# Context attention on 64-row halves with resident keys, and sums by a ones matmul

## The reference

```python
q = x_normed @ Wq + bq            # (2, 1024, 256), 16 heads of 16
k, v = ctx @ Wk + bk, ctx @ Wv + bv   # (2, 77, 256)
scores = q @ k.T / sqrt(16)       # first layer: k zeroed and a large negative number added where the mask is 0
p = softmax(scores, axis=-1)      # over 77 context tokens
out = (p @ v) @ Wo + bo
```

## Time and profile before

| | |
|---|---|
| Median of 3 runs | 3210.11 us (3195.41 to 3211.3) |
| The profiled execution | 3210.68 us, its span 3208.8 us |
| Stage `a1` | from 565.3 to 689.3 us |
| Stage `a4` | from 2064.4 to 2189.3 us |
| PE busy over the span | 2470.8 us, 77% |
| DVE busy over the span | 1611.6 us, 50% |
| ACT busy over the span | 1106.8 us, 34% |

### The profile page before, as it was taken

The page is one execution under the profiler, slowest core; times in us unless marked ns, Lnnn a source line. Parts: engine busy times, 40 slices in busy tenths (PEclk is TensorE's granted clock), DMA queues, the critical chain, the costliest instruction groups (busy, mean ns, idle before and its releaser), DMA issues. The chain is left out here.

```text
span 3208.8 us, 47429 instructions
## 1 busy us (share of the span) xinstructions
PE 2470.8 (77%) x16056; PEld 1352.3 (42%) x16056; DVE 1611.6 (50%) x2632; ACT 1106.8 (34%) x1993; POOL 923.3 (29%) x840
## 2 busy tenths in 40 slices
PE   4669975763899498799999996686479998419992
PEld 3524423332788375233333334544312222308882
DVE  3767725435223232566666662544679984412222
ACT  1326651330000133344444441142137887101110
POOL 0522232102000211477777772201612112030004
PEclk7969987575899799899999998767779999659996
DMA  3433213522565476122222213542432210154553
GB/s 106 100 71 84 70 25 76 87 56 85 182 208 184 132 194 179 64 83 81 80 83 81 84 59 106 104 80 71 101 58 62 59 36 16 43 174 165 194 190 111
DMA packets 280975, 322.77 MB, mean 101 GB/s; under 512 B 67470, under 2 KB 228148, under 8 KB 280308
## 3 DMA queue, kind: packets, MB, share of 16 engines
q1 hardware_dynamic: 252372, 257.75, 27.7%
q0 software_dynamic: 26528, 61.41, 8.1%
q10 hardware_dynamic: 1920, 1.57, 0.3%
HBM read 214.94 MB, written 104.88 MB: 100 GB/s over the span
## 5 line engine op out<-in xcount | busy, mean ns | idle before, releaser
L1673 DVE TENSOR_REDUCE a_mxw<-a_rows 128x2 f32<-128x1024 f32 (+1 forms) x448 | 480.5, 1105 | 111.9 <-PE a_rows L1529 63.8
L1648 ACT ACTIVATE a_probs<-a_cols 128x512 f32<-128x512 f32 (+3 forms) x896 | 445.8, 550 | 217.9 <-PE a_cols L1571 141.4
L2075 DVE TENSOR_REDUCE a_mxw<-a_rows 128x2 f32<-128x1024 f32 x256 | 313.3, 1224 | 209.2 <-PE a_rows L1913 207.4
L2053 ACT ACTIVATE a_probs<-a_cols 128x1024 f32<-128x1024 f32 x256 | 261.9, 1025 | 267.2 <-PE a_cols L1942 246.8
L1894 POOL TENSOR_TENSOR a_sums<-a_sums,a_probs 128x1024 f32<-128x1024 f32 x128 | 309.6, 2418 | 97.8 <-ACT a_probs L2053 84.8
L2384 PE MATMUL e_psU<-e_xT,e_w 128*128 128x256 f32 x1280 | 287.7, 383 | 18.9 <-DMA e_w<-in_w 10.0
L1571 PE MATMUL a_cols<-a_qs,a_ks 50*128 50x512 bf16 (+7 forms) x1792 | 280.9, 367 | 22.4 <-ACT a_probs L1648 11.5
L458 PE MATMUL t_psP<-t_xT,t_wf 128*128 128x256 f32 x1024 | 241.6, 393 | 35.1 <-ACT t_xT L526 13.0
L2384 PEld LDWEIGHTS e_psU<-e_xT,e_w 128*128 128x128 f32 x1280 | 244.1, 192 | 58.2 <-issue 24.8
L1938 PE MATMUL a_cols<-a_qf,a_kf 64*128 64x512 f32 x1024 | 266.8, 599 | 0.0
L1599 PE MATMUL a_out<-a_probs,a_vs 128*17 128x256 f32 (+4 forms) x3328 | 259.0, 385 | 0.2 <-ACT a_probs L1648 0.2
(11 more groups left out here) (229 smaller groups left out, 2930.0 us busy)
## 6 DMA issues: line engine op xcount, KB each, us to landing
e_w<-in_w SPq DMA_DIRECT2D x72, 512.0 KB
e_w<-in_w SPq DMA_DIRECT2D x32, 1024.0 KB
qk_wide_scratch<-t_f SPq DMA_DIRECT2D x32, 512.0 KB, 2.9
q_scratch<-t_parts POOLq DMA_DIRECT2D x128, 96.0 KB, 2.4
a_qs<-q_scratch SPq DMA_DIRECT2D x96, 128.0 KB
a_qs<-q_scratch SPq DMA_DIRECT2D x168, 64.0 KB, 2.5
sorted_scratch<-r_zero SPq DMA_DIRECT2D x40, 256.0 KB
e_xg<-sorted_scratch SPq DMA_DIRECT2D x40, 256.0 KB
```

Of the source, the lines that this page charges most:

```text
L1648: act.activation(pr[ug % RING][:, 2 * hp + e, c0:512], psC[(2 * at + e) % 3][:, 0:512 - c0], ACT.Exp, scale=scale).then_inc(ex_done, 1)
L1673: dve.tensor_reduce(mxw[w][:, a, :, hp, t % 4:t % 4 + 1], src[:, :, 0:n], AX.X, ALU.max).then_inc(s_free, 1)
L2053: act.activation(pr[i][:], psC[i % 2][:], ACT.Exp, scale=scale).then_inc(ex_done, 1)
L2075: dve.tensor_reduce(mxw[:, j % 2, :, j // 2:j // 2 + 1], psR[:], AX.X, ALU.max).then_inc(s_free, 1)
```

## The change

`attention_stage` goes, and `cross_attention_stage` takes its place in `a1` and `a4`.

- Keys, mask row and values of all 8 groups stay in SBUF from the start (`G["ctx_keys"]`, `G["ctx_values"]`). `context_loads` makes 15 transfers for `a1` and 13 for `a4`; SP issues all 28 in `t0` behind that stage's own loads (`later_loads`). POOL sets the rows of ones in stage `c`.
- The parts are split over two contractions on 64-row halves: 48 rows, with the mask row and two maximum rows (instead of three), and 48 more for the columns scores. Head e of a pair is on partitions 64e onwards. A pair of heads is a unit: `rows_step` is 8 matmuls into the single buffer `psR`, `cols_pair` is 4 matmuls of 512 columns into one of two `psC`, and one exp covers 77 x 1024.
- The sums are made by a second set of four matmuls, with ones as 32 stationary columns, into `psS`, so that each sum stands on all 32 rows of its head's strip. DVE then takes the reciprocal of 128 x 512 and multiplies `psO` by it (`divide`), once for each half of the queries. The copy to `osb`, both turns and ACT's last copy go. `psO` and `psS` have one bank each, and `values(g, w)` waits for the division before it (`o_done`).
- Query loads are six pieces of 64 KB on SP (those of the first contraction) and six on POOL (the rest). POOL stores a group in 4 transfers. SP's first load waits until 4 memsets of 32 x 2048 on DVE and 4 on POOL are done (`ones_set`).
- All 8 groups are written out, without a loop.

The diff, cut to its core; the lines of `attention_stage` that go are those printed above, all but a few left out here:

```diff
-                 ln2=None, x_loaded=None):
+                 ln2=None, x_loaded=None, later_loads=()):
...
+                        for dst, src, sem in later_loads:
+                            sp.dma_start(dst, src).then_inc(sem, 16)
...
+            def _(pool):
+                for l in range(NL):
+                    for e in range(2):
+                        pool.memset(G["ctx_keys"][l][64 * e + 32:64 * e + 64, 0], 1.0)
...
-def attention_stage(nc, G, tag, *, q, k, v, o, causal=False, cross=False, mask=None, sums=None):
...
+def context_loads(G, layer, k, v, mask):
+    kt, vt, sem = G["ctx_keys"][layer], G["ctx_values"][layer], G["ctx_loaded"][layer]
+    loads = []
+    for kind, parts in enumerate((CROSS_MAIN, CROSS_REST)):
+        for s, (_, part) in enumerate(parts):
+            for e in range(2):
+                rows = slice(64 * e + 16 * s, 64 * e + 16 * s + 16)
+                src = k.rearrange("i g b f s -> i (g b) f s")[part].rearrange("g (m e r) s -> e r (g m) s", e=2, r=16)[e]
+                loads.append((kt[rows, kind].rearrange("r g m s -> r (g m) s"), src, sem))
+    if mask is not None:
+        for e in range(2):
+            row = 64 * e + CROSS_MAX
+            loads.append((kt[row:row + 1, 0], mask.rearrange("g (m e) s -> e g m s", e=2)[e:e + 1], sem))
+    loads.append((vt[:], v.rearrange("g b p x -> p (g b) x"), sem))
+    return loads
+def cross_attention_stage(nc, G, tag, *, layer, q, o, masked, n_loads):
...
+    MAX_ROW = CROSS_MAX + masked
+    ROWS_K = [slice(64 * e, 64 * e + MAX_ROW) for e in range(2)]
+    MAIN_K = [slice(64 * e, 64 * e + MAX_ROW + 2) for e in range(2)]
+    REST_K = [slice(64 * e, 64 * e + CROSS_MAX) for e in range(2)]
...
+        qs = [st.sb(f"qs{p}", [P, 2, 2, 2, 512], BF16) for p in range(4)]
+        pr = [st.sb(f"probs{r}", [SC, 2, 512]) for r in range(RING)]
+        rec = [st.sb(f"rec{w}", [P, 512]) for w in range(2)]
+        psR = st.ps("rows", [P, 2, 512])
+        psC = [st.ps(f"cols{i}", [P, 2, 512]) for i in range(2)]
+        psO, psS = st.ps("out", [P, 512]), st.ps("sums", [P, 512])
...
+                def load(g):
+                    wait(sp, st_ready, 4 * (g - 3))
+                    for dst, src in loads_of(g, 0):
+                        sp.dma_start(dst, src).then_inc(main_ld[g % 4], 16)
+                def place(g):
+                    p = g % 4
+                    sp.wait_ge(mt_done, g + 1)
+                    for e in range(2):
+                        for i in range(2):
+                            row = 64 * e + MAX_ROW + i
+                            sp.dma_start(qs[p][row:row + 1, 0].rearrange("p w m (t q) -> p (w m t) q", q=P),
+                                         nparts[g % 2][TR // 2 * e:TR // 2 * (e + 1), i, :]).then_inc(mld[g % 2], 16)
+                sp.wait_ge(ones_set, 2)
+                load(0)
+                load(1)
+                place(0)
+                load(2)
+                for g in range(NG):
+                    if g + 1 < NG:
+                        place(g + 1)
+                    if g + 3 < NG:
+                        load(g + 3)
...
+                for p in (1, 3):
+                    for e in range(2):
+                        ins = pool.memset(qs[p][64 * e + 32:64 * e + 64, 0], 1.0)
                     pool.drain()
...
+                def rows_step(g, j):
+                    p, w, m = g % 4, j // 2, j % 2
+                    if j == 0:
+                        pe.wait_ge(main_ld[p], 16 * n_ld * (g // 4 + 1))
                         wait(pe, mt_done, g)
+                    wait(pe, s_free, 4 * g + j)
+                    for t in range(QT // 2):
+                        for e in range(2):
+                            mm = pe.matmul(psR[:, e, t * SC:(t + 1) * SC], qs[p][ROWS_K[e], 0, w, m, t * P:(t + 1) * P],
+                                           keys[ROWS_K[e], 0, g, m, :], start=True, stop=True)
                     mm.then_inc(s_ready, 1)
+                def turn_max(g):
+                    pe.wait_ge(s_free, 4 * (g + 1))
+                    pe.transpose(psR[0:TR, 0, 0:P], mx[:].rearrange("p e w m t -> p (e w m t)"), G["ident"][:]
+                                 ).then_inc(mt_ready, 1)
+                def cols_pair(g, n):
+                    p, w, m = g % 4, n // 2, n % 2
+                    at = 4 * g + n
+                    dst = psC[at % 2]
+                    if n == 0:
+                        pe.wait_ge(rest_ld[p], 16 * n_ld * (g // 4 + 1))
+                        pe.wait_ge(mld[g % 2], 16 * 4 * (g // 2 + 1))
+                    wait(pe, ex_done, at - 1)
+                    for e in range(2):
+                        pe.matmul(dst[0:SC, e, :], keys[MAIN_K[e], 0, g, m, :], qs[p][MAIN_K[e], 0, w, m, :],
+                                  start=True, stop=False)
+                    for e in range(2):
+                        mm = pe.matmul(dst[0:SC, e, :], keys[REST_K[e], 1, g, m, :], qs[p][REST_K[e], 1, w, m, :],
+                                       start=False, stop=True)
                     mm.then_inc(st_ready, 1)
+                def values(g, w):
+                    u = 2 * g + w
+                    pe.wait_ge(ex_done, 2 * (u + 1))
+                    wait(pe, o_done, u)
+                    for m in range(2):
+                        for e in range(2):
+                            at, pair = 32 * (2 * m + e), pr[(2 * u + m) % RING]
+                            pe.matmul(psS[at:at + 32, :], G["ones"][0:SC, 0:32], pair[:, e, :], start=True, stop=True)
+                    for m in range(2):
+                        for e in range(2):
+                            h = 2 * m + e
+                            mm = pe.matmul(psO[32 * h:32 * h + hd + 1, :], values_of[:, g, (hd + 1) * h:(hd + 1) * (h + 1)],
+                                           pr[(2 * u + m) % RING][:, e, :], start=True, stop=True)
+                    mm.then_inc(pv_done, 1)
+                pe.wait_ge(G["ctx_loaded"][layer], n_loads)
+                for j in range(4):
+                    rows_step(0, j)
+                turn_max(0)
+                rows_step(1, 0)
+                rows_step(1, 1)
+                pe.wait_ge(out_zeroed, 1)
+                for g in range(NG):
+                    cols_pair(g, 0)
+                    if g + 1 < NG:
+                        rows_step(g + 1, 2)
+                    cols_pair(g, 1)
+                    if g + 1 < NG:
+                        rows_step(g + 1, 3)
+                    if g:
+                        values(g - 1, 1)
+                    if g + 1 < NG:
+                        turn_max(g + 1)
+                    cols_pair(g, 2)
+                    if g + 2 < NG:
+                        rows_step(g + 2, 0)
+                    cols_pair(g, 3)
+                    if g + 2 < NG:
+                        rows_step(g + 2, 1)
+                    values(g, 0)
+                values(NG - 1, 1)
...
+                for n in range(4 * NG):
+                    act.wait_ge(st_ready, n + 1)
+                    wait(act, pv_done, (n - RING) // 2 + 1 if n >= RING else 0)
+                    act.activation(pr[n % RING][:], psC[n % 2][0:SC], ACT.Exp, scale=scale).then_inc(ex_done, 1)
...
+                for p in (0, 2):
+                    for e in range(2):
+                        ins = dve.memset(qs[p][64 * e + 32:64 * e + 64, 0], 1.0)
+                ins.then_inc(ones_set, 1)
                 dve.memset(psO[:], 0.0).then_inc(out_zeroed, 1)
-                def divide(g):
...
-                    dve.reciprocal(inv_q[:], turned[:, :, :, hd:hd + 1])
...
+                def maximum(g, j):
+                    w, m = j // 2, j % 2
+                    dve.wait_ge(s_ready, 4 * g + j + 1)
+                    if j == 0:
+                        wait(dve, mt_ready, g)
+                    view = psR[:, :, 0:QT // 2 * SC].rearrange("p e (t s) -> p e t s", s=SC)
+                    dve.tensor_reduce(mx[:, :, w, m, :], view, AX.X, ALU.max).then_inc(s_free, 1)
+                def negate_max(g):
+                    parts = nparts[g % 2]
+                    dve.wait_ge(mt_ready, g + 1)
+                    wait(dve, mld[g % 2], 16 * 4 * (g // 2))
+                    dve.tensor_scalar(parts[:, 0, :], psR[0:TR, 0, 0:P], -1.0, None, ALU.mult)
                     dve.drain()
+                    dve.scalar_tensor_tensor(parts[:, 1, :], psR[0:TR, 0, 0:P], -1.0, parts[:, 0, :],
+                                             ALU.mult, ALU.subtract).then_inc(mt_done, 1)
+                def divide(g, w):
+                    dve.wait_ge(pv_done, 2 * g + w + 1)
+                    wait(dve, stored[g % 3], g // 3 * H * 16)
+                    dve.reciprocal(rec[w][:], psS[:])
                     dve.drain()
+                    dve.tensor_tensor(on[g % 3][:, 512 * w:512 * (w + 1)], psO[:], rec[w][:], ALU.mult
+                                      ).then_inc(o_done, 1)
+                for j in range(4):
+                    maximum(0, j)
```

(20 more changed lines are left out.)

418 lines of the change are left out of this document (47 added, 371 removed).

## The result

| | Median, us | Runs | Against the kernel before |
|---|---|---|---|
| Before, same session | 3204.65 (3195.41 to 3211.3) | 4 | |
| After | 3343.11 (3340.15 to 3344.55) | 4 | 1.0426, 95% interval 1.0405 to 1.0447 |

A forecast was written before the change was run, and what follows sets the result against it. Bound before: PE's array work at its granted clock. A stage of 189 us at the lower clock, 156 at the higher, blended to 181.5, is 57 more than now; twice that on 3210.7 gives 3325 us, range 3268 to 3360.

The forecast's parts named there:

- Turns: Context stages: PE and DVE alternate over single `psR`, `psO` and `psS`, so their times add; a rows-and-maximum round takes 1.6 us.
- idle time of 1 to 2 us ahead of the sums: Sign in the changed profile: PE idle before the sums matmuls, put down to DVE's maximum or division, each time.
- The reciprocal: DVE's division: 128x512 reciprocal priced at 3.3 us from three smaller sizes, a division at 4.1 us.
- Rival (b): DVE's reciprocal costs eight cycles an element: 4.4 us each, 18 us more a stage, 3360 us in all; chance 0.08.
- A regular group: One group inside a context stage: 20.0 us at the lower clock, 16.0 at the higher, against 14.1 and 9.7 before.
- Start and end: Ends of a context stage: first rows step at 13.6 us, first columns at 25.0, end 5.9 us.
- The clock: PE's granted clock in the context stages stays at 0.61 to 0.62, giving 181.5 us between 189 and 156.
- the case that I had counted to the forecast as 3340: Part of rival (a): both context stages wholly at the lower clock level, program 3340 us.
- the two ends, 3274 and 3340: Rival (a), clock settles in the context stages: all higher gives 3274 us, chance 0.12; all lower gives 3340.
- Context loads and unrolling at nothing: 28 loads on SP, 12.6 us of issue, hide in `t0`; unrolling removes register instructions outside any wait; no cost.
- Rival (c): Engines overlap in the context stages: 14.9 us a group at the lower clock, program 3252 us; chance 0.04.
- Rival (d): Reciprocal of 512 as cheap as a plain 0.69 us, clock rises: stage 114 us, program 3190 us; chance 0.03.

The follow-up runs named there:

- experiment 5: Changed kernel with two `psO` and two `psS` buffers, one `psC`, and `values` ahead of the rows step: 3284.25 us, 1.0252 of the kernel before.
- experiment 1: Changed kernel with each 128x512 reciprocal replaced by a plain multiplication by 0.03: 3258.16 us, 1.0149 of the kernel before.
- 2: Changed kernel without the matmuls with ones, `psS` set once to a constant 30: 3289.57 us, 1.0241 of the kernel before.
- experiment 7: Changed kernel's resident keys, halves and pairs, but the old division by transposes, two `psO`, one `psC`, no sums: 3230.49 us, 1.009 of the kernel before.
- experiment 4: Changed kernel with the last group's four stores of each stage issued by SP instead of POOL: 3324.47 us, 1.0357 of the kernel before.
- 6: Changed kernel with two `psR` buffers and one `psC`, `psO` and `psS` still single: 3326.46 us, 1.0384 of the kernel before.
- 7 to 12: Kernels dividing by transposes, the later ones adding start, end, load-order or filler changes: 3230.49, 3209.11, 3199.21, 3194.68, 3203.14 and 3189.64 us.
- experiment 3: Changed kernel with six unread bf16 matmuls added twice a group in PE's pauses: 3301.86 us, 1.0281 of the kernel before.
- experiment 9: Transposes kernel with shortened start and end, plus SP issuing query loads ahead of placing the maxima: 3199.21 us, 0.9955 of the kernel before.
- experiment 11: Kernel of experiment 9 plus 14 unread matmuls before the first rows step and 8 before the first columns: 3203.14 us, 0.9981 of the kernel before.

## Why the prediction was right

I forecast 3325 us in a range of 3268 to 3360; it was 3343, slower as forecast, 133 us over the 3210.11 of before where I had 115 (138.5 over the same session's median, 129.8 from profile to profile). The mechanism, two engines that take turns over single buffers and a wide reciprocal in the chain, is what the runs show; part of the number's closeness is luck, as said below. By the steps of the prediction:

- **Turns.** Right, and shown: 5 takes 31 us off a stage with the same work, by buffers and an earlier place of `values`, and 1 and 2 show that work of either engine is paid in full. DVE is busy for 100.8 us a stage, as I had asked for (over 90). One sign did not come as I wrote it: I had asked for idle time of 1 to 2 us ahead of the sums, and in a regular group PE stands for 2.84 and 3.35 us ahead of the rows step. My own working gives this: division and maximum, 4.95 us, less 2.1 of columns scores.
- **The reciprocal.** 3349 ns for the 3.3 us that I took from the slope of three small sizes; a division is 4.1 us (650.01 to 654.1). Rival (b) is out. With experiment 7's 128x16 in 250 ns, it is (3349 - 250) / 496 = 6.2 ns for each further element. The Trainium skill's repeat count of 8 ("VectorE: DVE Perf Modes", "Walkthrough: the 8-slice pipeline in each mode"), read as eight cycles for each element at the 0.96 GHz of its page "Trainium Kernel Development and Optimization" ("NeuronCore Architecture"), would be an estimate of 4.3 us. The trace does not agree with that reading: it has 3.35 us.
- **A regular group.** 18.8 us for my 20.0. Some 0.7 of the 1.2 is the price of a rows step: 0.37 us to the next work (645.07 to 645.44) where I had 0.74, the "half too high" that I had allowed for. The rest is small differences in the values, the division, the turn and the negation. Sums take 1.70 us and values 1.87, against 1.84 each.
- **Start and end.** Both mis-sized. First rows step 16.6 us in, not 13.6: SP begins 9.0 us in and not 7.4, since DVE's four memsets with their gaps end last (573.30), and from there to the step it is 7.65 us and not 6.2; why the loads land later, with 24 of POOL's under way, was not separated. The end is 11.8 us and not 5.9; I had added three issues to the end of a stage with one store, and experiment 4 shows that the end with four stores on POOL costs 7 us more than on SP. Part of it comes even with one store on POOL (8.3 us in experiment 7, 4.3 before); the cause stays open. Over a stage these errors cancel by luck: first columns 3.1 us later and end 5.9 longer than priced, against 8 us less than priced for the eight groups between them. The sum at the lower clock was 189 us, and it is 189.7.
- **The clock.** This term decided my error. I blended in a share of the higher clock as before (181.5 us), and there was none at all; the case that I had counted to the forecast as 3340 is the one that came. What decides it stays open. In the profiles both stages are at 0.50 from end to end in every kernel with neither transposes nor filler (the change, 1, 2, 4, 5 and 6), and for a part at the higher level in each with transposes (before, 7 to 12); what in them does it was not tested. Filler in PE's pauses lifts the stage to 0.74 (experiment 3), but with pauses of at most 0.68 us in the regular groups it was 0.50 all the same (experiment 1). So even my argument for the lower end, PE idle through half of each division, is not borne out by itself. A point between two ends that no row decides was a guess; the two ends, 3274 and 3340, were the better statement.
- **Context loads and unrolling at nothing.** Right: `a1` begins 0.9 us earlier than before.

Rival (c), that the engines overlap, is what experiment 5 builds: a group of 14.5 us for my 14.9, and 3284 us for my 3252, at a clock of 0.50 and not the 0.61 of before, and with the longer start and end. Rival (d) is false even at the price it asked for.

## What to carry to other kernels

A division by row sums that turns the outputs so that queries lie on partitions needs one reciprocal for each query and head; spreading sums over rows by a matmul saves the transposes but makes DVE invert the same number many times over. Count elements on a partition, not instructions. And before moving work to an engine with idle time, look at what it shares with the engine that waits: with single buffers between them their times add up, and both look half idle. Here a second pair of buffers, with the order changed to use it, was worth 31 us a stage, and the dearer division 43 while the engines took turns; what that division costs once they overlap was not measured.

## What the hardware showed that I had not expected

- Useless matmuls in TensorE's pauses made the kernel 41 us faster (3343 to 3302), by a granted clock of 0.74 and 0.71 instead of 0.50 in the two stages.
- At the same code the level is not the same from run to run: experiment 9 had whole-program clocks from 0.859 to 0.876, with 3203.6 and 3165.47 us. 28.1 of 30 us busy in the regular groups without the higher level (experiment 1), and over 90% busy for 70 us until it came (experiment 11), are both in the traces. What sets the moment stays open.
- Four stores on POOL kept the stage from ending for 11.8 us after the last result, against 4.9 with the same four on SP. With one store on POOL it was 8.3 us in experiment 7 and 4.3 in the kernel before.
